# Inverse roots of two layer norms, moved from GpSimd's power to ScalarE's logarithm and exponential with a Newton step on VectorE

## The chip, the cores and the metric

The kernel runs on one core of one Trainium2 chip. The metric is device time in microseconds (us), the median of several runs; less is better. Engines go by the names of the profile: PE (TensorE), PEld (its weight loads), DVE (VectorE), ACT (ScalarE), POOL (GpSimd), SP (SyncE). L714 is line 714 of the kernel before.

## The reference

One decoder block without causal mask on 8 sequences of 512 tokens, width 192, in float32:

```python
params = quantum_params[token_ids.reshape(-1)]        # gather: 36 angles per token
ev = _circuit_expvals(params)                         # 6-qubit circuit, 6 expectations
h = (ev @ post_w.T + post_b).reshape(b, s, -1)
h = h + attention(_layernorm(h), W_qkv, b_qkv)        # one head, softmax over 512 keys
h = h + experts(_layernorm(h), Wg, W1, b1, W2, b2)    # top 2 of 8 experts, hidden 384, exact gelu
# _layernorm(x) = (x - mean) / sqrt(var + 1e-5)
```

Two layer norms per token are computed, so two inverse roots 1 / sqrt(var + 1e-5) per token are wanted.

## The kernel before, in words

A token's embedding is a linear map of 6 expectations, so the kernel never forms it for attention: it works with 7 to 15 numbers per token ("features") and small matrices that are folded from the weights at the start. Tokens lie 128 to a tile; there are 32 tiles, 4 per sequence (a "batch" b of 0 to 7). Two chunks of 16 tiles (batches 0 to 3 and 4 to 7) go through the circuit.

**The start.** POOL gathers the angles, one indirect DMA per tile (`gather_angles`, L542): 16 tiles for chunk 0, later 16 for chunk 1 in pieces. DVE reduces the angles, ACT takes sine and cosine (`trig`, three pieces p), DVE (chunk 0) or DVE and POOL (chunk 1, `pair_strings` on POOL) multiply the circuit out to `ev`.

**First norm.** Per chunk c, `variance1(c)` on DVE leaves var + eps in `ve1` (L1173, semaphore `var1_done`). POOL's `rstd1(p)` raises it to the power -0.5 (L714), in four parts p of 4, 12, 4 and 12 tiles. DVE's `features(p)` waits for that (`rs1_done`), scales and writes `u` and `w`, from which PE makes keys (`keys`), queries and the factor (`factor`, waits for `w_done`) of the batch. Ahead of `features(0)` DVE computes `form(0, 0, E)` (L1156, L1160), which needs no root.

**Attention.** Per batch and half h, PE multiplies scores (L1862 for maxima, L1855 transposed for the softmax), DVE takes maxima (`row_max`, L1191), ACT exponentiates (`softmax`, L1593), PE multiplies the context (L1874), DVE divides (`context`).

**Second norm and routing.** Per batch, `variance2(b)` on DVE copies PE's gram product (L1240, semaphore `t2_copied`) and leaves `ve2` (L1248). For batches 0 to 2 (`POWERS` is 3) POOL's `rstd2(b)` raises it to -0.5 (L718); for batches 3 to 7 DVE starts from a bit trick and takes three Newton steps (`route_and_root`, with `root_square`, `root_scale`, `root_next` at L1272, L1275, L1278). `normed(b)` uses the root (L1339, L1340), ACT's `gap_exponent` and DVE's `shares(b)` give the gates (L1220, `gates_done`), and POOL scatters 8 tiles of rows per batch to HBM by indirect DMA (`scatter`, L725), batch after batch.

**Experts.** SP loads 71 blocks of 128 rows back, PE multiplies up (L2084) and down (L2096), ACT applies gelu (L1720) and the share (L1732), POOL scatters each block's result (L770), SP loads the sums, DVE adds them.

The order on each engine is the order of the calls, written out by hand; each engine runs its queue in order, and a wait holds all that is behind it. On POOL the order around the change is: 4 gathers, `last_string(0)`, 7 gathers, `rstd1(0)`, `rstd1(1)`, 5 gathers, `pair_strings(1)` with `rstd2(0)` inside it, then the scatters of batch 0 with `rstd1(2)`, `rstd1(3)` between them, `rstd2(1)` ahead of its second half and `rstd2(2)` in batch 1, then all other scatters, then the 71 scatters of results. PE's `residual(0, 0)` (L1941), which stands ahead of scores of batches 4 and 5 in PE's queue, waits for `t2_copied` to reach 4, which is `variance2(3)`.

## Time and profile before

| what | value |
|---|---|
| median of 3 runs | 297.35 us |
| lowest and highest run | 296.71 and 297.77 us |
| span of the profiled execution | 294.9 us |
| busy share of the span: PE, DVE, ACT, POOL | 72%, 59%, 41%, 71% |

The span is the time from the first to the last instruction of the one execution that the profiler recorded; no separate time of that execution is given. The median of the runs is 2.45 us above the span; that is taken as what lies around it. Busy shares are averages over stages with different limits: the start, attention with routing (about 55 to 160 us), and the experts (160 us to the end).

### The profile page before, as it was taken

What the parts mean: (1) busy time and instruction counts of PE and PEld (TensorE: products, weight loads), DVE (VectorE), ACT (ScalarE), POOL (GpSimd) and SP (SyncE); (2) the same over time, 40 slices, a digit from 0 to 9 for tenths busy, and PEclk for the clock granted to TensorE, in tenths of its full rate; (3) what the DMA queues carried; (4) which work ended last, traced back from release to release, by engine and by line L of the source; (5) the groups of instructions that cost most, each with busy time, mean ns of one, the idle gap of its engine ahead of it and who ended that gap; (6) DMA issues with size and microseconds to landing.
All of it is one profiled execution on the core that took longest, in us unless ns stands there. A gap on an engine that the chain in (4) does not pass through costs nothing.

```text
span 294.9 us, 5764 instructions
## 1 busy us (share of the span) xinstructions
PE 211.9 (72%) x1552; PEld 150.7 (51%) x1552; DVE 175.2 (59%) x687; ACT 121.3 (41%) x292; POOL 210.2 (71%) x281
## 2 busy tenths in 40 slices
PE   0760699367864678977689598999999999988000
PEld 0540554122431434544356387878789989867000
DVE  5754999756899989595887757784211000842122
ACT  2002013135351331356533467667665766745000
POOL 5777786740899697877776776777777777777750
PEclk9999999655596655579855779999999999999655
DMA  7811003994000000000012221022333315997454
GB/s 166 278 18 15 1 3 118 397 328 163 2 0 0 4 9 11 13 13 17 14 22 47 60 45 26 16 85 86 100 101 89 96 67 175 370 364 234 111 222 161
DMA packets 25659, 29.86 MB, mean 101 GB/s; under 512 B 15130, under 2 KB 19473, under 8 KB 25435
## 3 DMA queue, kind: packets, MB, share of 16 engines
q1 hardware_dynamic: 19148, 21.54, 23.3%
q0 software_dynamic: 6480, 7.94, 8.8%
q8 instruction: 14, 0.23, 0.4%
q14 instruction: 17, 0.14, 0.2%
HBM read 14.13 MB, written 16.02 MB: 102 GB/s over the span
## 4 chain that ended last, share of the span: by engine, by line
PE 47%; DVE 21%; POOL 12%; issue 7%; ACT 7%; DMA 4%; POOLq 1%; DVEq 0%; SPq 0%; ACTq 0%
PE bank_b L2096 24%; PE bank_a L2084 6%; POOL circuit L542 5%; PE bank_b L1855 4%; PE bank_a L1862 3%; POOL shares_out L770 3%; DVE nmax L1191 3%; POOL rs L714 2%; PE bank_c L1874 2%; ACT prob L1593 2%; POOL routed L725 1%; DMA angle_stages<-shares_out 1%; PE bank_d L1958 1%; DVE circuit L883 1%; DMA shares_out<-circuit,up 1%
## 5 line engine op out<-in xcount | busy, mean ns | idle before, releaser
L770 POOL DMA_INDIRECT shares_out<-circuit,up x71 | 72.6, 1023 | 21.6 <-issue 16.5
L2096 PE MATMUL bank_b<-wide,up 128*128 x426 | 81.0, 339 | 2.8 <-ACT up L1720 1.2
L725 POOL DMA_INDIRECT routed<-rows,slot x64 | 63.3, 989 | 23.5 <-issue 18.9
L2096 PEld LDWEIGHTS bank_b<-wide,up 128*128 128x128 f32 x426 | 69.7, 194 | 9.9 <-issue 8.3
L1732 ACT ACTIVATE circuit<-bank_b,up 128x192 f32<-128x192 f32 x71 | 29.9, 421 | 25.0 <-PE bank_b L2096 23.4
L542 POOL DMA_INDIRECT circuit<-angles,ids x32 | 31.3, 978 | 10.8 <-issue 9.0
L1720 ACT ACTIVATE up<-bank_a 128x384 f32<-128x384 f32 x71 | 34.5, 489 | 6.9 <-PE bank_a L2084 6.9
L1862 PE MATMUL bank_a<-keys_t,wt 32*128 32x512 f32 x64 | 27.8, 956 | 4.7 <-DVE nmax L1191 3.0
L1855 PE MATMUL bank_b<-queries_t,keys_t 32*128 32x512 f32 x64 | 24.6, 850 | 6.2 <-ACT keys_t L1571 3.5
L1518 DVE TENSOR_TENSOR hres<-hres,prob 128x384 f32<-128x384 f32 x12 | 6.2, 559 | 37.8 <-DMA prob<-shares_out 37.7
L1191 DVE TENSOR_REDUCE nmax<-bank_a 128x2 f32<-128x1024 f32 x16 | 19.5, 1220 | 11.3 <-PE bank_a L1862 11.3
L1540 DVE COPY up<-wide 32x384 f32 x43 | 17.0, 395 | 12.6 <-PE bank_a L2084 8.3
L1593 ACT ACTIVATE prob<-bank_b 128x1024 f32<-128x1024 f32 x16 | 16.4, 1023 | 16.3 <-PE bank_b L1855 16.3
L2084 PE MATMUL bank_a<-xt,up 32*128 32x128 f32 x330 | 14.7, 309 | 1.4 <-ACT up L1720 1.3
L2084 PEld LDWEIGHTS bank_a<-xt,up 32*128 32x128 f32 x330 | 12.2, 205 | 5.3 <-issue 5.0
L1559 ACT ACTIVATE circuit<-angle_stages 128x480 f32<-128x480 f32 (+2 forms) x3 | 2.3, 780 | 28.3 <-DVE angle_stages L839 28.3
L1874 PE MATMUL bank_c<-prob,u 128*32 128x128 f32 x256 | 12.9, 366 | 0.7 <-ACT prob L1593 0.5
L1874 PEld LDWEIGHTS bank_c<-prob,u 128*32 128x32 f32 x256 | 9.5, 146 | 4.9 <-issue 2.3
L1540 DVE COPY circuit<-wide 32x384 f32 x16 | 6.2, 385 | 9.4 <-PE bank_a L2084 4.7
L1855 PEld LDWEIGHTS bank_b<-queries_t,keys_t 32*128 32x128 f32 x64 | 7.0, 251 | 9.1 <-issue 7.7
L1567 ACT COPY wide<-bank_a 128x384 f32<-128x384 f32 x8 | 3.8, 478 | 18.2 <-PE bank_a L1800 18.2
L1862 PEld LDWEIGHTS bank_a<-keys_t,wt 32*128 32x128 f32 x64 | 7.1, 267 | 7.4 <-issue 4.8
(433 smaller groups left out, 392.9 us busy)
## 6 DMA issues: line engine op xcount, KB each, us to landing
routed<-pad_rows SPq DMA_DIRECT2D x8, 528.0 KB, 5.2
out<-hres SPq DMA_DIRECT2D x7, 384.0 KB, 6.0
wide<-down_w SPq DMA_DIRECT2D x1, 2304.0 KB, 12.6
prob<-shares_out SPq DMA_DIRECT2D x3, 768.0 KB, 5.4
up<-up_w SPq DMA_DIRECT2D x1, 1536.0 KB
angle_stages<-shares_out SPq DMA_DIRECT2D x2, 768.0 KB, 7.0
form_p<-shares_out SPq DMA_DIRECT2D x2, 768.0 KB, 7.1
up<-routed SPq DMA_DIRECT2D x71, 16.0 KB, 1.7
```

The lines of the kernel that those rows point to most:

```text
L542: pool.indirect_dma_start(out=theta_all[:, t, :], out_offset=None, in_=angles, in_offset=bass.IndirectOffsetOnAxis(ids[:, b, j:j + 1], 0)) ...
L725: pool.indirect_dma_start(out=routed, out_offset=bass.IndirectOffsetOnAxis(slot[:, b, k, j:j + 1], 0), in_=rows[:, b, k, j, :], in_offset=None
L770: pool.indirect_dma_start(out=shares_out, out_offset=bass.IndirectOffsetOnAxis(xb[:, m, DEST:DEST + 1].bitcast(I32), 0), in_=y[:, m % RESU ...
L1191: dve.tensor_reduce(nmax[:, b % 2, 2 * h:2 * h + 2], bank_a[:, 0:2, :], AX.X, ALU.max, negate=True).then_inc(max_done, 1)
L1540: copied = dve.tensor_copy(up_now[s % UP_TILES][r, :], wide_flat[r, bass.ds(first + HC * D, HID)])
L1720: act.activation(hid[:, n, :], bank_a[:, n, 0:HID], ACT.Gelu).then_inc(gelu_done, 1)
L1732: act.mul(y[:, m % RESULTS, :], bank_b[:, m % 2, 0:D], xb[:, m, SHARE:SHARE + 1]).then_inc(y_done, 1)
L1855: mm = pe.matmul(bank_b[:, n, :], keys_t[r, bt % 3, k * P:(k + 1) * P], queries_t[r, :], start=True, stop=True)
L1862: mm = pe.matmul(bank_a[:, n, :], wt[r, bs % 2, :], keys_t[r, bs % 3, :], start=True, stop=True)
L1874: mm = pe.matmul(bank_c[j * F:(j + 1) * F, 0:P], u[:, b * TILES + k, :], prob[:, k, j * P:(j + 1) * P], start=(k == 0), stop=(k == TILES - 1),
L2084: mm = pe.matmul(bank_a[:, n, c * P:(c + 1) * P], weights[r, c * P:(c + 1) * P], xt[r, 0, :], start=True, stop=True)
L2096: mm = pe.matmul(bank_b[:, m % 2, 0:D], hid[:, m % STEP, c * P:(c + 1) * P], wide_flat[:, bass.ds(first + c * D, D)], start=(c == 0), stop ...
```

## The change

POOL's powers go (`rstd1`, `rstd2`, `minus_half`). ACT gets `root1(c)`, once per chunk, and `root2(b)` for batches 0 to 2: the logarithm of var + eps, then exp(-0.5 of it). DVE gets functions of the same names that wait for ACT's value and take one Newton step of three chained instructions each. The gathers of chunk 1 on POOL now stand in one run of 12. ACT loads a table set with both functions after `trig(0)` and after `trig(2)`.

```diff
             gather_angles(COUNT[0], COUNT[0] + GATHERS_EARLY)
             join()
             constants()
             last_string(0)
-            gather_angles(COUNT[0] + GATHERS_EARLY, ANGLE_LAST[1])
-            rstd1(0)
-            rstd1(1)
-            gather_angles(ANGLE_LAST[1], T)
-            pair_strings(1, lambda: rstd2(0))
+            gather_angles(COUNT[0] + GATHERS_EARLY, T)
+            pair_strings(1)
             pool.wait_ge(pads_out, 16 * (E + 1))
             for b in range(BATCHES):
-                if b == 0:
-                    scatter(0, 0, 0, 2)
-                    rstd1(2)
-                    scatter(0, 0, 2, TILES)
-                    rstd1(3)
-                else:
-                    scatter(b, 0)
-                if b + 1 < POWERS:
-                    rstd2(b + 1)
+                scatter(b, 0)
                 scatter(b, 1)
...
+            def root1(c):
+                n = COUNT[c]
+                dve.wait_ge(rs1_done, c + 1)
+                step(dve.tensor_tensor(square1[:, 0:n], rs1[:, 0:n], rs1[:, 0:n], ALU.mult))
+                join()
+                step(dve.scalar_tensor_tensor(square1[:, 0:n], square1[:, 0:n], -0.5, ve1[:, 0:n], ALU.mult, ALU.mult))
+                join()
+                step(dve.scalar_tensor_tensor(rs1[:, 0:n], square1[:, 0:n], 1.5, rs1[:, 0:n], ALU.add, ALU.mult))
+                join()
...
+            def root2(b):
+                dve.wait_ge(rs2_done, b + 1)
+                root_square()
+                join()
+                root_scale()
+                join()
+                root_next()
...
             form(0, 0, E)
+            root1(0)
             features(0)
...
             route(0)
+            root2(0)
             normed(0)
...
             form(1, 0, E)
+            root1(1)
             features(2)
             route(1)
             features(3)
+            root2(1)
             normed(1)
...
             row_max(5, 0)
+            root2(2)
             normed(2)
...
+            def root1(c):
+                n = COUNT[c]
+                act.wait_ge(var1_done, c + 1)
+                act.activation(log1[:, 0:n], ve1[:, 0:n], ACT.Ln).then_inc(log1_done, 1)
+                act.wait_ge(log1_done, c + 1)
+                act.activation(rs1[:, 0:n], log1[:, 0:n], ACT.Exp, scale=-0.5).then_inc(rs1_done, 1)
...
             trig(0)
+            act.preload_act_table_set("natural_log_exp_and_others")
             for e in range(E):
                 up_copy(e)
+            root1(0)
             spread_u(0)
...
                     trig(2)
+                    act.preload_act_table_set("natural_log_exp_and_others")
...
             at_copy(1)
+            root2(0)
             softmax(2, 1)
...
             softmax(3, 0)
+            root1(1)
             at_copy(2)
+            root2(1)
             softmax(3, 1)
...
             context_copy(3)
+            root2(2)
```

How the order moves on DVE at the first norm, before (L1173 is `variance1`'s last step, L1156 and L1160 are `form(0, 0, E)`, L1182 opens `features(0)` and then `features(1)`):

```order
L1173 TENSOR_SCALAR ve<-var_s 128x16 [waits dve_step]
L1156 TENSOR_TENSOR form_p<-ev,form_w 128x16x56
L1160 TENSOR_REDUCE form_s<-form_p 128x16x8 [waits dve_step]
L1182 TENSOR_TENSOR u<-ev,rs 128x4x7 [waits rs1_done,dve_step]
L1184 TENSOR_TENSOR form_s<-form_s,rs 128x4x8
L1186 TENSOR_TENSOR w<-form_s,form_w 128x4x8 [waits dve_step]
L1182 TENSOR_TENSOR u<-ev,rs 128x12x7 [waits rs1_done]
```

and now:

```order
L1154 TENSOR_SCALAR ve<-var_s 128x16 [waits dve_step]
L1137 TENSOR_TENSOR form_p<-ev,form_w 128x16x56
L1141 TENSOR_REDUCE form_s<-form_p 128x16x8 [waits dve_step]
L1160 TENSOR_TENSOR square<-rs 128x16 [waits rs1_done,dve_step]
L1162 SCALAR_TENSOR_TENSOR square<-square,ve 128x16 [waits dve_step]
L1164 SCALAR_TENSOR_TENSOR rs<-square,rs 128x16 [waits dve_step]
L1173 TENSOR_TENSOR u<-ev,rs 128x4x7 [waits dve_step]
L1175 TENSOR_TENSOR form_s<-form_s,rs 128x4x8
L1177 TENSOR_TENSOR w<-form_s,form_w 128x4x8 [waits dve_step]
L1173 TENSOR_TENSOR u<-ev,rs 128x12x7
```

Three chained instructions now stand ahead of `features(0)`, and `features(1)` waits for no other engine any more.

On DVE at batch 2, before (two maxima L1191 and the copy L1198 between them, then `normed(2)`, then L1240, the copy of `variance2(3)`):

```order
L1191 TENSOR_REDUCE nmax<-bank_a 128x2 [waits s_done]
L1198 COPY w_rep<-nmax 128x16 [waits queries_done,max_done]
L1191 TENSOR_REDUCE nmax<-bank_a 128x2 [waits s_done]
L1339 TENSOR_TENSOR gap<-gap,rs 128x4 [waits rs2_done]
L1340 TENSOR_TENSOR rows<-ev,rs 128x8x15
L1240 COPY t<-bank_a 128x96 [waits t2_done]
```

and now:

```order
L1182 TENSOR_REDUCE nmax<-bank_a 128x2 [waits s_done]
L1189 COPY w_rep<-nmax 128x16 [waits queries_done,max_done]
L1182 TENSOR_REDUCE nmax<-bank_a 128x2 [waits s_done]
L1263 TENSOR_TENSOR square<-rs 128x4 [waits rs2_done]
L1266 SCALAR_TENSOR_TENSOR scaled<-square,ve 128x4 [waits dve_step]
L1269 SCALAR_TENSOR_TENSOR rs<-scaled,rs 128x4 [waits dve_step]
L1336 TENSOR_TENSOR gap<-gap,rs 128x4 [waits dve_step]
L1337 TENSOR_TENSOR rows<-ev,rs 128x8x15
L1231 COPY t<-bank_a 128x96 [waits t2_done]
```

The Newton step of batch 2 stands ahead of the copy that `residual(0, 0)` on PE waits for.

On ACT around the second piece of angles, now (before, the list is the same without the row ACT_TABLE_LOAD and without `log` and `rs`):

```order
L1629 ACTIVATE log<-ve 128x16 [waits var1_done]
L1631 ACTIVATE rs<-log 128x16 [waits log1_done]
L1614 COPY u_rep<-u 128x16x9 [waits u_done]
L1577 COPY wt<-bank_a 128x128 [waits wt_done]
L1573 COPY keys_t<-bank_d 128x512 [waits keys_done]
L1561 ACT_TABLE_LOAD
L1561 ACTIVATE circuit<-angle_stages 128x30x11 [waits reduced]
```

The table load of the sine stands ahead of the wait for the angles (`reduced`), so it may run while that wait is still open.

## Rows read from the trace of the kernel before

**Rows 1.** The page, part 4: chain that ended last, by engine.

```profile
PE 47%; DVE 21%; POOL 12%; issue 7%; ACT 7%; DMA 4%; POOLq 1%; DVEq 0%; SPq 0%; ACTq 0%
```

**Rows 2.** Lines L714 and L718: count, ns min/median/max, first and last start.

```profile
L714 POOL TENSOR_TENSOR rs<-ve,minus_half x4: 1051/2048/2304, 52.7 to 107.0; 128x4 f32<-128x4 f32 x2, 128x12 f32<-128x12 f32 x2
...
L718 POOL TENSOR_TENSOR rs<-ve,minus_half x3: 997/1042/1044, 94.0 to 120.4; 128x4 f32<-128x4 f32 x3
```

**Rows 3.** Timeline, POOL: start us, us, what, [idle before and its releaser].

```profile
158.81 0.95 POOL L725 DMA_INDIRECT routed<-rows,slot  x1 [1.73 <-DVE ev L1220]
...
179.91 0.97 POOL L725 DMA_INDIRECT routed<-rows,slot  x1 [1.22 <-issue]
...
283.78 1.22 POOL L770 DMA_INDIRECT shares_out<-circuit,up  x1 [0.30 <-issue]
```

**Rows 4.** Timeline, DVE: the last instruction of two batches' shares.

```profile
157.81 0.19 DVE L1220 TENSOR_TENSOR ev<-shared 128x32 f32<-128x32 f32 x1
...
178.92 0.19 DVE L1220 TENSOR_TENSOR ev<-shared 128x32 f32<-128x32 f32 x1
```

**Rows 5.** Timeline, DVE: a Newton step by itself, and the instruction behind it.

```profile
129.53 0.16 DVE L1272 TENSOR_TENSOR square<-rs 128x4 f32<-128x4 f32 x1
129.73 0.16 DVE L1275 SCALAR_TENSOR_TENSOR scaled<-square,ve 128x4 f32<-128x4 f32 x1
...
130.12 0.16 DVE L1339 TENSOR_TENSOR gap<-gap,rs 128x4 f32<-128x4 f32 x1
```

**Rows 6.** Timeline, ACT.

```profile
59.80 0.80 ACT L1559 ACTIVATE circuit<-angle_stages 128x330 f32<-128x330 f32 x1 [2.45 <-DVE angle_stages L839]
...
71.35 1.28 ACT L1593 ACT_TABLE_LOAD   x1
...
96.65 0.20 ACT L1628 ACTIVATE gap_e<-gap 128x4 f32<-128x4 f32 x1
```

**Rows 7.** Timeline, DVE, first norm of chunk 0.

```profile
49.83 0.98 DVE L1156 TENSOR_TENSOR form_p<-ev,form_w 128x784 f32<-128x784 f32 x1
...
52.55 1.08 DVE L1156 TENSOR_TENSOR form_p<-ev,form_w 128x896 f32<-128x896 f32 x1
...
54.79 0.19 DVE L1182 TENSOR_TENSOR u<-ev,rs 128x28 f32<-128x28 f32 x1
...
56.84 0.25 DVE L1182 TENSOR_TENSOR u<-ev,rs 128x84 f32<-128x84 f32 x1 [1.51 <-POOL rs L714]
...
60.22 1.22 DVE L1191 TENSOR_REDUCE nmax<-bank_a 128x2 f32<-128x1024 f32 x1
```

**Rows 8.** Timeline, PE: the first scores.

```profile
57.40 2.08 PE L1862 MATMUL bank_a<-keys_t,wt 32*128 32x512 f32 x4 [0.67 <-ACT keys_t L1571]
```

**Rows 9.** Timeline, DVE, first norm of chunk 1 and batch 1.

```profile
108.20 0.22 DVE L1268 TENSOR_REDUCE both<-both 128x8 bf16<-128x40 bf16 x1
109.30 0.25 DVE L1182 TENSOR_TENSOR u<-ev,rs 128x84 f32<-128x84 f32 x1 [0.88 <-POOL rs L714]
...
110.28 0.16 DVE L1339 TENSOR_TENSOR gap<-gap,rs 128x4 f32<-128x4 f32 x1 [0.20 <-POOL rs L718]
...
113.23 1.21 DVE L1191 TENSOR_REDUCE nmax<-bank_a 128x2 f32<-128x1024 f32 x1
```

**Rows 10.** Timeline, PE: scores behind that maximum, and the residual of batch 0.

```profile
114.59 2.08 PE L1862 MATMUL bank_a<-keys_t,wt 32*128 32x512 f32 x4 [0.89 <-DVE nmax L1191]
...
121.35 1.06 PE L1835 MATMUL bank_d<-ident,w_rep 128*128 128x128 f32 x4
122.48 1.01 PE L1941 MATMUL bank_a<-m,a2t 32*128 32x192 f32 x4
```

**Rows 11.** Timeline, DVE: the copy of the second norm of batch 3.

```profile
122.13 0.25 DVE L1240 COPY t<-bank_a 128x96 f32<-128x96 f32 x1
```

**Rows 12.** Timeline, POOL and DVE side by side.

```profile
90.46 1.70 POOL L688 TENSOR_TENSOR pair_e<-pair_e,turn 128x720 f32<-128x720 f32 x1
90.51 1.76 DVE L1084 TENSOR_TENSOR z_exp<-z_exp,circuit 128x96 f32<-128x96 f32 x1
```

More of the change, by code:

```diff
@@ L74, in build @@
     FEATURE_LAST = [sum(FEATURE_BATCHES[:p + 1]) for p in range(len(FEATURE_BATCHES))]
-    POWERS = CHUNK_BATCHES[0] - 1
+    GUESSED = CHUNK_BATCHES[0] - 1
     USED = ANGLES - QUBITS
@@ L153, in build @@
         ones_b = sb("ones_b", [P, P], BF16)
-        minus_half = sb("minus_half", [P, CT])
         exp_i = sb("exp_i", [P, E], I32)
@@ L202, in build @@
         rs1 = sb("rs1", [P, CT])
+        log1 = sb("log1", [P, CT])
+        square1 = sb("square1", [P, CT])
+        log2 = sb("log2", [P, TILES])
         w = sb("w", [P, T, F])
@@ L314, in build @@
         rs1_done = sem("rs1_done")
+        log1_done = sem("log1_done")
+        log2_done = sem("log2_done")
         u_done = sem("u_done")
@@ L544, in gather_angles @@
                                             ).then_inc(angles_in[p], 16)
-            step(pool.memset(minus_half[:, :], -0.5))
             pool.wait_ge(ids_in, 16)
@@ L608, in last_string, with pair_strings @@
                 pool.tensor_tensor(of(x_exp, n)[:, 5], lc[:, 0, 0], lc[:, 0, 1], ALU.add).then_inc(last_done, 1)
-            def pair_strings(c, between):
+            def pair_strings(c):
                 n = COUNT[c]
@@ L694, in pair_strings @@
                 pjoin()
-                between()
                 pool.tensor_tensor(d[:, :, 0], g[:, :, 0, 0], s[:, :, 1], ALU.add)
@@ L708, in pair_strings @@
                 pool.tensor_tensor(x, x, sin_of(c, 2, 0), ALU.mult).then_inc(pairs_done, 1)
-            def rstd1(p):
-                c, first, last = part_tiles(p)
-                own = slice(first - TILE0[c], last - TILE0[c])
-                pool.wait_ge(var1_done, c + 1)
-                pool.tensor_tensor(rs1[:, own], ve1[:, own], minus_half[:, own], ALU.pow).then_inc(rs1_done, 1)
-            def rstd2(b):
-                pool.wait_ge(var2_done, b + 1)
-                pool.tensor_tensor(rs2[:, :], ve2[:, :], minus_half[:, 0:TILES], ALU.pow).then_inc(rs2_done, 1)
             def scatter(b, k, first=0, last=TILES):
@@ L1180, in features @@
                 scale = rs1[:, own].unsqueeze(2)
-                dve.wait_ge(rs1_done, p + 1)
                 dve.tensor_tensor(u[:, tiles, 0:PU], ev[:, tiles, 0:PU], scale.to_broadcast([P, n, PU]), ALU.mult
@@ L1334, in normed @@
             def normed(b):
-                if b < POWERS:
-                    dve.wait_ge(rs2_done, b + 1)
-                else:
-                    join()
+                join()
                 dve.tensor_tensor(gap_2[:, :], gap[:, :], rs2[:, :], ALU.mult).then_inc(gap_done, 1)
@@ L1622, in spread_w, with root2 @@
                          ).then_inc(w_spread, 1)
+            def root1(c):
[4 more added lines that the diff above has]
+                act.activation(rs1[:, 0:n], log1[:, 0:n], ACT.Exp, scale=-0.5).then_inc(rs1_done, 1)
+            def root2(b):
+                act.wait_ge(var2_done, b + 1)
+                act.activation(log2[:, :], ve2[:, :], ACT.Ln).then_inc(log2_done, 1)
+                act.wait_ge(log2_done, b + 1)
+                act.activation(rs2[:, :], log2[:, :], ACT.Exp, scale=-0.5).then_inc(rs2_done, 1)
             def gap_exponent(b):
```

## Prediction

> **What bounds the kernel now.** I read the page's chain of waits first. It gives POOL 12% of the span [rows 1], and much of that share in its middle belongs to the powers that the change removes. That invites a large gain, so the next view is the powers' own lines: seven of them, 1.0 to 2.3 us each [rows 2]. But a long instruction on POOL costs only what somebody waits for it, so the third view is DVE's timeline, where the users of the roots stand. DVE idled for a power 1.51 us at `features(1)` [rows 7], 0.88 us at `features(3)` and 0.20 us at `normed(1)` [rows 9]. The other four powers end before their users come. That is 2.59 us in all: the stock from which a gain can come.
>
> The second thing to see is how the end is set. The last scatter of results starts at 283.78 us and the first scatter of batch 7 at 179.91 [rows 3]; 8 + 71 scatters in 103.9 us, 78 steps of 1.33 us, and the timeline shows none of them idle for more than about 0.3 us ahead. So from 179.91 on POOL itself is the limit. What lets it begin is DVE: the shares of batch 7 end at 178.92 + 0.19 = 179.11 [rows 4], and the scatter follows 0.80 us later. Batch 5 shows the same with the releaser named: shares end at 158.00 [rows 4], scatter at 158.81 after 1.73 us of idle [rows 3]. POOL is therefore waiting for the attention path at 158 and again at 179. Time that the powers free on POOL around 103 to 121 us only makes these waits longer. What counts is how far the path DVE, PE, ACT through attention shifts.
>
> **The change part by part.** All positions are those of the profiled execution, span 294.9 us; the median of the runs is 2.45 us above, which I carry over unchanged.
>
> *The new steps.* A Newton step standing by itself: first instruction at 129.53, the instruction behind it at 130.12 [rows 5], so 0.59 us for three chained instructions. The width (16 instead of 4 columns for the first norm) adds at most some hundredths. Lower bound: the three busy times of about 0.16 us without gaps, 0.48 us. Upper bound: one of the steps held by POOL as in [rows 12], where an instruction of 96 columns took 1.76 us beside a POOL instruction of 1.70 us. I take 0.59, from the row of the very same instructions. There are five steps, 2.95 us of DVE.
>
> *ACT's pair.* The trace shows no logarithm. The nearest row is an exponential of 4 columns, 0.20 us [rows 6]; the upper bound is a sine of 330 columns, 0.80 us [rows 6]. I take 0.20 each, by width, and about 0.5 us for the pair with its hand-over. Cover at the first norm: the power starts at 52.7 [rows 2], so the pair can start there and be done by 53.3 (54.4 at the upper bound), while DVE works without a gap until 54.79 [rows 7]. Free. Were the cover gone, `features(0)` would pay the 0.5 us. In chunk 1 and for batches 0 to 2 the pair stands in ACT's queue at a place where its input is ready within half a microsecond, and DVE reads the result microseconds later (route and features lie between), so it is free there too; behind it wait small copies and a softmax that itself waits for PE.
>
> *Tables.* Two more loads. One row costs 1.28 us [rows 6]. The one after `trig(0)` falls into an empty ACT. The sine's load falls behind the first key copy, which ends just ahead of the first scores [rows 8], so at about 58.0 us now, and ACT idled 2.45 us at this place for the angles [rows 6]; 58.0 + 1.28 is before the 59.8 at which the sine starts now. Free. The load after `trig(2)` takes the place of the one at 71.35, same length. Zero.
>
> *Gathers in one run.* The last five, issued from 57 us on, now come without the pause; DVE does not wait for any gather there, before or after. Zero. POOL's pair products start when DVE allows it, as before. Zero.
>
> *First norm, chunk 0.* DVE's Newton step delays `features(0)` from 54.79 to 55.38. PE's factor, keys and first scores follow: 57.40 becomes 57.99, ending 2.08 later at 60.07 [rows 8]. On the other side `features(1)` starts at 56.84 - 1.51 + 0.59 = 55.92 [rows 7], 0.92 us early, and with it the reduction of angles, so DVE would be ready for the first maximum at 60.22 - 0.92 = 59.30 [rows 7]. The maximum needs both: about 60.1 instead of 60.22. **-0.1 us.** The 1.51 us of waiting is nearly all lost again: DVE now waits for PE.
>
> *Chunk 1 and batches 0, 1.* Between about 82 and 113 us the timeline shows no idle time of DVE but the two waits, so it is the path. Three steps come in (`root2(0)`, `root1(1)`, `root2(1)`): 3 x 0.59 = 1.77. Two waits go: 0.88 + 0.20 = 1.08 [rows 9]. **+0.7 us** at the maximum of 113.23 [rows 9]. PE idles 0.89 us for just that maximum before 114.59 [rows 10]; PE's own work there is later by two steps, 1.2 us, so it would be ready at 114.9, and the maximum allows 115.2. DVE stays the last, and the shift passes on.
>
> *Batch 2.* `root2(2)` stands ahead of the copy at 122.13 + 0.25 = 122.38 [rows 11]. PE is free for the residual at 121.35 + 1.06 = 122.41 and starts it at 122.48 [rows 10]: there is no slack, and scores of batches 4 and 5 are queued behind it. The step passes on whole. **+0.6 us.** The power it replaces was not waited for.
>
> *POOL.* Four powers leave the stretch of scatters, but the waits of [rows 3] take that in. **0.**
>
> Sum: -0.1 + 0.7 + 0.6 = +1.2 us. Everything behind 122 us is chained to that residual, the same as before. 294.9 + 1.2 is 296.1 of span, 298.5 us of time.
>
> Waits are not all that a power can cost DVE. The product of 896 columns beside the first power took 1.08 us, that of 784 columns without any POOL arithmetic 0.98 us [rows 7], 1.21 and 1.25 ns a column; a power of a few columns does not slow DVE visibly. [rows 12] show that a wide POOL product does. The Trainium skill, page "Advanced Engine Details and Errata", section "VectorE Performance Modes", says that VectorE's second port to SBUF is shared with GPSIMD and that the two block each other. By that rule, with the powers holding the port, taking them away would free DVE time as well; what it gives is the first rival. The row at 52.55 disagrees with it for these narrow powers, the row at 90.51 agrees for a wide one.
>
> **The rivals.**
>
> 1. *Faster: the powers hold DVE.* In chunk 1 powers of 1.05 and 2.30 us [rows 2] run beside DVE work; less the 0.88 us in which DVE idled anyway, up to 2.5 us of DVE could come back there. +1.2 - 2.5 = -1.3: about 296.1 us. For it: [rows 12]. Against it: the two rates in [rows 7]. It decides if DVE's instructions from 103 to 109 us run clearly shorter than before.
> 2. *Absorbed.* One of the two shifts meets slack that I do not see: the residual's scores matter less than the maxima of batch 5, or PE hides a part at 114.6. Then only +0.6: 297.9 us, no measurable change. For it: margins of 0.1 to 0.3 us in my comparisons. Against it: PE idles for DVE in [rows 10].
> 3. *Slower still: a Newton step is held by POOL.* `root2(0)` comes at about 96 us while POOL's pair products still run. A hold as at 90.51 [rows 12], 1.76 us where a product of 84 columns takes 0.25 [rows 7], so 1.5 us, would give +2.7: 300.0 us. It decides if one of the new instructions shows far above 0.2 us. Against it: the wide product is over by then.
>
> That the change does not do what it says is excluded by the order of instructions.
>
> **How the numbers follow.** A measurement of this kernel tells about 0.3%, 0.9 us, from no change: the bounds are 296.5 and 298.2 us. My forecast has 0.50, with its own range 297.8 to 299.2 (steps of 0.48 to 0.7 us, and 0.5 us for the spread of the runs): 0.35 of it slower, 0.15 the same. Rival 1 has 0.18: 0.15 faster, 0.03 the same. Rival 2 has 0.17: 0.16 the same, 0.01 slower. Rival 3 has 0.15, all slower. Together: faster 0.15, same 0.34, slower 0.51. The range from 296.4 to 300.0 leaves out most of rival 1 and the outer part of rival 3, under 2 in 10.
>
> **What would show it.** Right: `features(1)` no longer waits, but the first maximum stands at 60.1 with DVE idle ahead of it for PE; the pair on ACT done by 53.3 and 0.2 us each; five Newton steps of 0.6 us; the maximum of 113.23 about 0.6 later, the residual of batch 0 about 1.2 later, the first scatter of batch 7 about 181.1, POOL's idle time ahead of the scatters of batches 1, 2 and 5 larger; from there the same 79 scatters. Wrong: the first maximum a microsecond early, DVE's instructions beside the former powers shorter, the residual not behind the copy, or another start of batch 7 than the path says.

## The result and the profile after

The changed kernel took 298.81 us in the median of 4 runs (298.08 to 301.14); the kernel before, run beside it on the same chip, 297.03. The ratio on record is 1.0101, with a 95% interval of 1.0052 to 1.0150 (it is taken over the executions and is not the quotient of these two medians, 1.006). Measured once more (label new_again below) it is 1.0111 (1.0068 to 1.0154). By the means of this study, over 11 executions of the changed kernel and 145 of the kernel before, it is 299.43 against 296.28 us: **+3.1 us**. Executions more than 1.5% above the fastest of the same kernel count as disturbed and are left out of every mean here. The forecast was +1.2, and 298.5 in all. The direction was right and the time lies in the range; the size of the change was forecast at well under half. That 298.81 lies so near 298.5 is in part luck: the forecast started from a median of three, 297.35, which is 1.1 us above the mean of the 145, and this hid half of the miss.

The page of the changed kernel; compare the chain with [rows 1]. The third line is TensorE's granted clock in 40 slices of 7.4 us (9 is full, 5 is half).

```profile
PE 209.3 (70%) x1552; PEld 150.1 (50%) x1552; DVE 178.2 (60%) x702; ACT 125.9 (42%) x304; POOL 200.4 (67%) x273
...
PEclk9999997555975755559955579999999999999655
...
PE 48%; DVE 26%; POOL 8%; issue 7%; ACT 6%; DMA 4%; POOLq 0%; DVEq 0%; SPq 0%; ACTq 0%
```

POOL's share of the chain fell from 12% to 8%: the powers have left it, and yet the kernel is slower. The span of this execution is 297.6 us and its time 299.32, so 1.72 us lie around the span. That is also so in the other executions (1.72 to 1.76 us in the mean of each kernel). The prediction took 2.45, the median less the span of one execution, and so started 0.7 us too high.

The first norm on DVE, which answers to [rows 7] (start, length, engine, line, operation, tiles, count, idle time before it and its releaser):

```profile
52.41 1.08 DVE L1137 TENSOR_TENSOR form_p<-ev,form_w 128x896 f32<-128x896 f32 x1
...
54.65 0.18 DVE L1160 TENSOR_TENSOR square<-rs 128x16 f32<-128x16 f32 x1
54.87 0.18 DVE L1162 SCALAR_TENSOR_TENSOR square<-square,ve 128x16 f32<-128x16 f32 x1
55.08 0.18 DVE L1164 SCALAR_TENSOR_TENSOR rs<-square,rs 128x16 f32<-128x16 f32 x1
55.29 0.19 DVE L1173 TENSOR_TENSOR u<-ev,rs 128x28 f32<-128x28 f32 x1
...
55.75 0.24 DVE L1173 TENSOR_TENSOR u<-ev,rs 128x84 f32<-128x84 f32 x1
...
60.03 1.22 DVE L1182 TENSOR_REDUCE nmax<-bank_a 128x2 f32<-128x1024 f32 x1 [0.65 <-PE bank_a L1884]
```

The step takes 55.29 - 54.65 = 0.64 us; `features(1)` (55.75) waits for nothing, and the first maximum stands at 60.03 with DVE idle for PE. This is what the prediction said, to a tenth. ACT's side of it, for the first norm (and the sine's table load, which was to come at 58.0):

```profile
52.54 0.22 ACT L1629 ACTIVATE log<-ve 128x16 f32<-128x16 f32 x1 [4.73 <-DVE ve L1154]
52.79 0.22 ACT L1631 ACTIVATE rs<-log 128x16 f32<-128x16 f32 x1
...
57.88 1.28 ACT L1561 ACT_TABLE_LOAD   x1
```

The pair is done at 53.01. The load hides in ACT's wait for the angles but for some 0.3 us: DVE has the angles ready at 58.85 now, and the sine starts at 59.17, still 0.63 earlier than in [rows 6]. Now chunk 1, batches 0 and 1 on DVE, against [rows 9], with the POOL row beside the first of them:

```profile
95.02 0.70 DVE L1269 SCALAR_TENSOR_TENSOR rs<-scaled,rs 128x4 f32<-128x4 f32 x1
...
108.49 0.23 DVE L1173 TENSOR_TENSOR u<-ev,rs 128x84 f32<-128x84 f32 x1
...
109.18 0.15 DVE L1263 TENSOR_TENSOR square<-rs 128x4 f32<-128x4 f32 x1
...
109.56 0.16 DVE L1269 SCALAR_TENSOR_TENSOR rs<-scaled,rs 128x4 f32<-128x4 f32 x1
109.76 0.16 DVE L1336 TENSOR_TENSOR gap<-gap,rs 128x4 f32<-128x4 f32 x1
...
112.47 1.22 DVE L1182 TENSOR_REDUCE nmax<-bank_a 128x2 f32<-128x1024 f32 x1
```

```profile
95.01 0.69 POOL L703 TENSOR_TENSOR pair_d<-pair_d,turn 128x240 f32<-128x240 f32 x1
```

Both waits for powers are gone. The maximum of batch 4 stands at 112.47, 0.76 us earlier than in [rows 9], where the prediction had 0.6 later. And the third instruction of `root2(0)` takes 0.70 us instead of 0.16, beside a POOL product of 0.69. Last, PE's residual, against [rows 10], and POOL's first scatters of batches 5 and 7, against [rows 3]:

```profile
122.32 0.69 PE L1963 MATMUL bank_a<-m,a2t 32*128 32x192 f32 x2 [0.65 <-issue]
```

```profile
160.74 0.96 POOL L717 DMA_INDIRECT routed<-rows,slot  x1 [1.67 <-DVE ev L1211]
...
182.48 0.98 POOL L717 DMA_INDIRECT routed<-rows,slot  x1 [1.67 <-issue]
```

The residual stands 0.16 us earlier than in the first trace of before, the first scatter of batch 7 is 2.57 us later (182.48 against 179.91). Most of the loss thus shows behind the place where the prediction had stopped counting. From the first scatter of batch 7 to the last scatter of results it is 104.06 us, against 103.87 before, so next to nothing is lost there. One recorded execution of each kernel does not tell whether that is the change or the execution, so both were recorded again.

### The profile page after: what moved, and what is told of

Same layout as the page of the kernel before. It is cut to its first block, busy times and chain, and to the rows that moved or that the text cites. A ratio compares the mean times of both kernels' runs of the same rounds, so it can differ in the third digit from the quotient of the medians.

```text
span 297.6 us, 5781 instructions
## 1 busy us (share of the span) xinstructions
PE 209.3 (70%) x1552; PEld 150.1 (50%) x1552; DVE 178.2 (60%) x702; ACT 125.9 (42%) x304; POOL 200.4 (67%) x273
## 4 chain that ended last, share of the span: by engine, by line
PE 48%; DVE 26%; POOL 8%; issue 7%; ACT 6%; DMA 4%; POOLq 0%; DVEq 0%; SPq 0%; ACTq 0%
PE bank_b L2118 24%; PE bank_a L2106 6%; POOL circuit L546 5%; PE bank_a L1884 4%; PE bank_b L1877 4%; POOL shares_out L751 3%; DVE nmax L1182 3%; PE bank_c L1896 2%; DVE form_s L1141 1%; DVE circuit L864 1%; DVE form_p L1137 1%; PE bank_d L1835 1%; PE bank_d L1857 1%; DVE circuit L870 1%; DVE circuit L861 1%
## 5 line engine op out<-in xcount | busy, mean ns | idle before, releaser
L1884 PE MATMUL bank_a<-keys_t,wt 32*128 32x512 f32 x64 | 27.2, 935 | 3.3 <-ACT keys_t L1573 1.7
L1877 PE MATMUL bank_b<-queries_t,keys_t 32*128 32x512 f32 x64 | 23.9, 827 | 5.1 <-ACT keys_t L1573 2.7
L1182 DVE TENSOR_REDUCE nmax<-bank_a 128x2 f32<-128x1024 f32 x16 | 19.5, 1220 | 11.5 <-PE bank_a L1884 11.5
L1542 DVE COPY up<-wide 32x384 f32 x43 | 16.4, 381 | 12.8 <-PE bank_a L2106 8.3
L1896 PE MATMUL bank_c<-prob,u 128*32 128x128 f32 x256 | 13.7, 384 | 0.8 <-ACT prob L1595 0.7
L1847 PE MATMUL bank_a<-ident,w 128*128 128x128 f32 x8 | 3.4, 420 | 12.6 <-DVE w L1177 10.3
L1857 PE MATMUL bank_d<-ident,w_rep 128*128 128x128 f32 x32 | 7.5, 382 | 4.7 <-issue 4.7
```

The costliest lines, as they stand in the source:

```text
L1182: dve.tensor_reduce(nmax[:, b % 2, 2 * h:2 * h + 2], bank_a[:, 0:2, :], AX.X, ALU.max, negate=True).then_inc(max_done, 1)
L1542: copied = dve.tensor_copy(up_now[s % UP_TILES][r, :], wide_flat[r, bass.ds(first + HC * D, HID)])
L1877: mm = pe.matmul(bank_b[:, n, :], keys_t[r, bt % 3, k * P:(k + 1) * P], queries_t[r, :], start=True, stop=True)
L1884: mm = pe.matmul(bank_a[:, n, :], wt[r, bs % 2, :], keys_t[r, bs % 3, :], start=True, stop=True)
L1896: mm = pe.matmul(bank_c[j * F:(j + 1) * F, 0:P], u[:, b * TILES + k, :], prob[:, k, j * P:(j + 1) * P], start=(k == 0), stop=(k == TILES - 1),
```

## The experiments

L numbers are those of the kernel meant. "Mean" is over the executions of a kernel, with a standard error of 0.2 to 0.5 us; the kernel before has 296.28. The runs were spread over five chips, on which the kernel before had means of 296.1 to 296.6, so means of different chips are compared below.

| kernel | ratio to before, 95% interval | mean, us (executions) |
|---|---|---|
| old_again | 1.0012 (0.9984 to 1.0041) | with before |
| old_third | 0.9981 (0.9945 to 1.0016) | with before |
| new_again | 1.0111 (1.0068 to 1.0154) | 299.43 (11, with the first 4) |
| no_newton | 0.9961 (0.9927 to 0.9996) | 295.31 (12) |
| newton_twice | 1.0204 (1.0156 to 1.0252) | 302.80 (6) |
| only_first | 0.9994 (0.9965 to 1.0022) | 295.90 (12) |
| only_chunk1 | 1.0082 (1.0049 to 1.0114) | 298.29 (7) |
| only_batch2 | 0.9991 (0.9960 to 1.0022) | 295.87 (12) |
| only_batch0 | 0.9976 (0.9934 to 1.0019) | 295.76 (8) |
| only_root1_1 | 0.9995 (0.9962 to 1.0028) | 296.06 (12) |
| only_batch1 | 0.9965 (0.9932 to 0.9998) | 294.83 (12) |
| only_two | 0.9989 (0.9958 to 1.0020) | 296.01 (11) |
| root2_earlier | 1.0064 (1.0033 to 1.0096) | 297.80 (9) |
| old_with_steps | 1.0076 (1.0042 to 1.0110) | 298.47 (11) |
| idle_power | 1.0075 (1.0037 to 1.0114) | 298.75 (10) |
| log_for_more | 0.9936 (0.9898 to 0.9973) | 294.99 (12) |

### Both kernels again: old_again, new_again, old_third

No edit. What was expected, of old_again and new_again, and later of old_third:

> The kernel before, unchanged, measured against itself. All theories: ratio 1.000 within 0.003. What it tells is TensorE's granted clock: the profiled execution of the kernel before had 0.822 over its span, the changed one 0.806, and the changed one's trace loses 1.5 to 2 us between 122 and 175 us where the clock stands at its lower level for longer. Theory 'clock by chance': the executions of this kernel spread over 0.80 to 0.82, and those at about 0.805 are about 1.5 us longer. Theory 'clock by the kernel': all executions of this kernel lie at about 0.82.

> The changed kernel, unchanged, measured again. Theory 'steps alone' (what is lost is the Newton steps on VectorE's path, +1.2 us as forecast; the rest of the first measurement was chance of the executions): ratio 1.002 to 1.006, clocks spread as in the kernel before. Theory 'steps and clock' (the shifted work loses granted clock in every execution): ratio 1.008 to 1.012 again, clocks at 0.80 to 0.806 in nearly all.

> The kernel before once more, for the trace. Theory 'the waits for powers in chunk 1 were an accident of the first recorded execution': no idle time of VectorE for a power at features(3) and normed(1), as in the second one (there 0.20 us at normed(0) alone). Rival 'they are usual': 0.5 to 1.1 us of idle time there.

The change's loss came back whole (1.0111), so it is no chance of one measurement. Time at full clock, worked out per execution from its span and mean clock (the lower level counts 0.5, so it is the span times twice the clock less one), is 186 us in the mean of the kernel before (granted 0.799 to 0.828) and 182 in that of the changed one. That the kernel before always stands at 0.82 is wrong; it spreads, and its 25 executions at 0.806 or less took 297.6 us in the mean, the other 120 296.0. The seven of new_again lie at 0.806 to 0.812, above the 0.80 to 0.806 that 'steps and clock' had.

The theory of an accident fell with old_third. DVE in old_third, then in old_again, at the same place of the program:

```profile
94.93 0.32 DVE L1339 TENSOR_TENSOR gap<-gap,rs 128x4 f32<-128x4 f32 x1 [0.20 <-POOL rs L718]
...
108.56 0.25 DVE L1182 TENSOR_TENSOR u<-ev,rs 128x84 f32<-128x84 f32 x1 [0.87 <-POOL rs L714]
109.55 0.16 DVE L1339 TENSOR_TENSOR gap<-gap,rs 128x4 f32<-128x4 f32 x1 [0.20 <-POOL rs L718]
```

```profile
94.83 0.32 DVE L1339 TENSOR_TENSOR gap<-gap,rs 128x4 f32<-128x4 f32 x1 [0.20 <-POOL rs L718]
...
102.39 0.18 DVE L1204 RECIPROCAL rinv<-bank_c 128x4 f32<-128x4 f32 x1 [0.66 <-PE bank_c L1881]
```

Two of three recorded executions wait 1.07 or 1.08 us for the powers of these two places; the third does not, and 6 us earlier it has waited 0.66 us for PE's context. (The two later recordings also wait 0.20 us for a power at `normed(0)`, where the first trace has no wait.) Here is what differs: two stretches by engine, first in old_third, then in old_again (busy time and count of PE, PEld, DVE, ACT, POOL, then granted clock, DMA share, GB/s):

```profile
100.00:103.50 3.50, 2.39 (x14) 0.82 (x10) 3.23 (x11) 1.55 (x3) 3.00 (x3) 0.97 0.04 9
121.70:130.50 8.80, 6.66 (x40) 3.77 (x40) 7.72 (x47) 4.85 (x12) 6.67 (x8) 0.69 0.06 13
```

```profile
100.00:103.50 3.50, 2.74 (x8) 0.75 (x8) 2.60 (x9) 1.29 (x2) 2.98 (x4) 0.50 0.04 9
120.90:129.60 8.70, 6.49 (x40) 3.76 (x40) 7.62 (x47) 4.62 (x12) 6.57 (x8) 0.70 0.05 11
```

Around 101 us old_third had a short **bout at 2.4 GHz** (0.97), old_again ran at 1.2 (0.50). With the bout PE's context comes early and the power is what DVE waits for; without it DVE waits for PE first, and the power is done in time. All 18 recorded executions of this study bear this out: in none of the 8 with this bout does DVE wait for PE at that reciprocal, and in 9 of the 10 without it it waits 0.65 to 0.88 us. The 1.08 us of [rows 9] were worth that much only in executions with that bout. The second row of each is the stretch from `residual(0, 0)` to `row_max(6, 0)`: both have a bout in it. The same two stretches in the changed kernel, first the execution on the page, then new_again:

```profile
100.00:103.50 3.50, 2.59 (x22) 0.93 (x14) 3.23 (x12) 2.08 (x6) 2.89 (x3) 0.96 0.04 9
122.30:131.90 9.60, 7.42 (x40) 4.39 (x40) 7.42 (x47) 4.27 (x11) 5.17 (x7) 0.50 0.04 9
```

```profile
100.00:103.50 3.50, 2.93 (x17) 0.75 (x9) 2.46 (x8) 1.20 (x3) 2.89 (x3) 0.50 0.04 9
123.40:133.00 9.60, 7.44 (x40) 4.34 (x40) 7.44 (x48) 4.25 (x11) 5.17 (x7) 0.51 0.04 9
```

So with the early bout there are the first trace of before, old_third and the page of after; without it there are old_again and new_again. Cut at DVE's and PE's rows into stretches, A from `row_max(3, 0)` to `row_max(4, 0)`, B to `residual(0, 0)`, C to `row_max(6, 0)`, D to the end of `shares(7)`, in us:

| execution | A (bout near 101) | B | C (bout in it) | D (bout at 150 to 168) |
|---|---|---|---|---|
| before, first trace | 26.87 (yes) | 9.25 | 8.96 (yes) | 47.67 (yes) |
| old_third | 27.59 (yes) | 9.25 | 8.78 (yes) | 46.87 (yes) |
| old_again | 26.93 (no) | 8.88 | 8.74 (yes) | 46.96 (yes) |
| after, the page | 28.08 (yes) | 9.85 | 9.59 (no) | 49.77 (no) |
| new_again | 28.47 (no) | 9.84 | 9.60 (no) | 47.03 (yes) |
| no_newton | 26.16 (no) | 9.64 | 9.59 (no) | 49.11 (no) |
| only_two | 26.88 (yes) | 9.26 | 8.86 (yes) | 48.06 (yes) |

Where both have the bout, A costs +0.49 against old_third (28.08 - 27.59) and +1.21 against the first trace (28.08 - 26.87); where neither has it, +1.54 (28.47 - 26.93). Two executions of the same kernel with the bout differ by 0.72 themselves, so the bout alone does not set this cost. B costs +0.60 against the two traces without a bout in it. C is 9.59 us without a bout and 8.74 to 8.96 with one. D is 2 to 3 us longer in the page of after than in new_again or the kernel before; that execution has no bout there. In the mean of the recorded executions (three before, two after) the residual comes at 121.70 and 122.85, +1.15, and `shares(7)` ends at 177.69 and 180.84, +3.15.

### All steps out, or twice: no_newton, newton_twice

```diff
 def root1(c):
...
     dve.wait_ge(rs1_done, c + 1)
-    step(dve.tensor_tensor(square1[:, 0:n], rs1[:, 0:n], rs1[:, 0:n], ALU.mult))
...
 def root2(b):
...
     dve.wait_ge(rs2_done, b + 1)
-    root_square()
...
-    root_next()
```

newton_twice has these lines twice instead.

> The changed kernel without its five Newton steps: the roots are ScalarE's exponentials of -0.5 times the logarithm as they stand; the refinement is left out. Theory 'steps alone': first norm 0.65 us earlier than before the change (first maximum at about 59.55), the two waits of 0.88 and 0.20 us gone without steps in their place, batch 2 unchanged: 0.9 to 1.7 us faster than the kernel before, ratio 0.994 to 0.997. Theory 'clock' (what was lost behind 122 us doesn't hang on the steps): 0 to 1 us slower than before, ratio 1.000 to 1.004. Theory 'logarithm and tables on ScalarE': first maximum no earlier than before, ratio 1.003 or more.

> The changed kernel with each Newton step done twice, 2.95 us of VectorE more. Theory 'steps alone': chunk 0 +0.6, chunk 1 and batches 0 and 1 +1.8, batch 2 +0.6, together 2.4 to 3.0 us more than the changed kernel, ratio to the kernel before 1.012 to 1.016 if the changed one has 1.004. Theory 'clock': the shift passes 122 us as 2.4 to 3.0 but the end is off it by up to 2 us either way, with the granted clock.

Without steps the kernel is 1.0 us faster than before, at the near end of what was expected; the first maximum stands at 59.55, as expected to the hundredth. So no cost of the ACT pair, the tables and the gathers shows, and five steps cost 299.43 - 295.31 = 4.1 us where they are 2.95 us of DVE (error 0.5). The second five cost 3.4 more. That is above the 2.4 to 3.0 of 'steps alone' but within its error; 'clock' allowed it at the end, yet not that the shift is above 3.0 already at `residual(0, 0)`, which newton_twice has at 126.68 where the changed kernel has it at 122.32 and 123.37. The steps are the whole loss, and all five together cost more than themselves. That the rest of the gain from the waits was not to be had shows in DVE's rows of no_newton:

```profile
59.55 1.23 DVE L1176 TENSOR_REDUCE nmax<-bank_a 128x2 f32<-128x1024 f32 x1 [0.88 <-PE bank_a L1873]
...
101.35 0.18 DVE L1189 RECIPROCAL rinv<-bank_c 128x4 f32<-128x4 f32 x1 [0.65 <-PE bank_c L1892]
...
114.52 1.22 DVE L1176 TENSOR_REDUCE nmax<-bank_a 128x2 f32<-128x1024 f32 x1 [0.37 <-PE bank_a L1873]
```

A faster DVE waits for PE: 0.88 us for the first scores, 0.65 us for the context and 0.37 us for the scores of `row_max(4, 1)`.

### Steps one by one: only_first, only_batch2, only_chunk1

The edit puts a condition ahead of the step's lines, or takes them out where no step is wanted; only_first, for example (it has no step in `root2`):

```diff
 def root1(c):
...
     dve.wait_ge(rs1_done, c + 1)
-    step(dve.tensor_tensor(square1[:, 0:n], rs1[:, 0:n], rs1[:, 0:n], ALU.mult))
...
+    if c in (0,):
+        step(dve.tensor_tensor(square1[:, 0:n], rs1[:, 0:n], rs1[:, 0:n], ALU.mult))
...
```

> The changed kernel with the Newton step of chunk 0 alone; the other four are left out, so those roots are not refined. Without any step the first maximum came at 59.55 us, with all of them at 60.14. Theory 'each step costs itself': first maximum at 60.1, the whole 0.6 us longer than without any step, ratio to the kernel before 0.997 to 0.999. Theory 'clock' (a shift is turned into a larger or smaller one by the granted clock behind it): the shift at the first maximum is 0.6, at the end anything from -1 to +2, ratio 0.993 to 1.003.

> The changed kernel with the steps of chunk 1 and of batches 0 and 1 alone; chunk 0's and batch 2's are left out. Theory of the forecast (three steps of 0.59 less two waits of 1.08 us that a power really cost): +0.7 us against the kernel before less the 0.6 of chunk 0, so ratio 1.000 to 1.001. Theory 'the waits were an accident of the one recorded execution' (in the second recorded execution of the kernel before, features(3) and normed(1) wait for no power): the three steps cost 1.8 us and the 0.5 us for which a product on GpSimd holds one of them, so +2.3 us at the maximum of batch 4 against no step at all, some 0.4 of it hidden by TensorE behind it: ratio 1.002 to 1.004.

> The changed kernel with the Newton step of batch 2 alone; the other four are left out. Without any step the ratio was 0.996. Theory 'it passes on whole, once': +0.6 us at residual(0, 0) and at the end, ratio 0.997 to 0.999. Theory 'it is worth more than itself' (moving it ahead of row_max(5, 0) took 1.6 us off the changed kernel by the means of 9 and 11 executions): +1.6 us, ratio 1.000 to 1.003.

Chunk 0's step costs 295.90 - 295.31 = 0.6 us, batch 2's 0.6 us, as the forecast had them. The three of chunk 1 and of batches 0 and 1 cost 298.29 - 295.31 = 3.0 us (error 0.4): this is the term that was wrong, and more than either theory had for it. 0.6 + 0.6 + 3.0 = 4.2 agrees with the 4.1 of all five.

### The three apart: only_batch0, only_root1_1, only_batch1, only_two

The same edit with other conditions; only_two has `root1(1)` and `root2(1)`.

> The changed kernel with the Newton step of batch 0's second norm alone; the others are left out. Without any step the mean was 295.3 us. Theory 'the GpSimd product holds this step': third instruction 0.70 us, row_max(3, 1) 1.1 us later, mean 296.4 us, ratio 0.999 to 1.001. Rival 'each of the three costs the same third of 3.0 us': mean 296.3 us too, but then with 0.6 us at row_max(3, 1) and the rest behind it. Rival 'each costs itself, the excess comes when they add up': mean 295.9 us.

> The changed kernel with the Newton step of the first norm of chunk 1 alone; the others are left out. Theory 'the excess is the product on GpSimd, at batch 0 alone': +0.6 us against no step, mean 295.9 us, ratio 0.997 to 0.999. Rival 'each of the three costs a third of 3.0 us': mean 296.3 us. TensorE would still be free to hide some: 0.4 us of slack stood behind the maximum of batch 4 without steps, so +0.2 us is possible.

> The changed kernel with the Newton step of batch 1's second norm alone; the others are left out. Theory 'the excess is the product on GpSimd, at batch 0 alone': +0.2 to 0.6 us against no step, mean 295.5 to 295.9 us, ratio 0.996 to 0.999. Rival 'each of the three costs a third of 3.0 us': mean 296.3 us.

> The changed kernel with the Newton steps of the first norm of chunk 1 and of batch 1's second norm alone; the other three are left out. Theory 'each costs itself, once': mean between 295.6 us (the sum of the two single runs) and 296.5 us (twice 0.59 on no step), ratio 0.996 to 0.999, time at full clock 184 to 186 us. Theory 'two steps in one stretch lose a bout of the full clock': mean 297.0 us or more, ratio 1.001 to 1.004, time at full clock 180 to 183 us, and from row_max(3, 1) to row_max(4, 0) 17.5 us without a bout at about 100 us, where one step alone shows 16.1.

The hold is there in only_batch0. Its DVE row and the POOL row beside it:

```profile
94.53 0.69 DVE L1263 SCALAR_TENSOR_TENSOR rs<-scaled,rs 128x4 f32<-128x4 f32 x1
```

```profile
94.52 0.69 POOL L703 TENSOR_TENSOR pair_d<-pair_d,turn 128x240 f32<-128x240 f32 x1
```

`row_max(3, 1)` comes 1.1 us after that of no_newton, as the theory of the hold said; in the time it makes +0.5 us where that theory had 1.1, from only 8 of 12 executions (all 12 would make it +1.3). only_root1_1 costs 0.75, as expected; only_batch1 -0.5, where 0.2 to 0.6 was expected and the error is 0.5; only_two 0.7: two steps in one stretch cost no more than themselves, and the theory that they lose a bout fell. Batch 0 alone and these two make 0.5 + 0.7 = 1.2 us, the three together 3.0, and the error of that difference is about 0.7; with all 12 executions of only_batch0 and of only_two the excess would be 0.6 and not 1.8. So it is not settled whether the three together cost more than their sum, and where an excess would lie the single steps don't show.

### The product moved away: idle_power

Two fills of constants at the start, for the power's operands, are left out here:

```diff
 pjoin()
+pool.tensor_tensor(idle_p[:, 0:TILES], idle_p[:, CT - TILES:CT], minus_half[:, 0:TILES], ALU.pow)
 pool.tensor_tensor(d[:, :, 0], g[:, :, 0, 0], s[:, :, 1], ALU.add)
```

> The changed kernel with one idle power of 4 columns on GpSimd at the place in pair_strings where the kernel before had that of batch 0; nobody waits for its result. In the changed kernel the third instruction of root2(0) takes 0.70 us beside a GpSimd product of 240 columns (0.69 us); in the kernel before the power of 1.06 us put that product 1.1 us later. Theory 'the product holds the step': with the power back, the third instruction takes about 0.2 us, row_max(3, 1) starts 0.5 us earlier, and the whole is about 0.5 us faster than the changed kernel, ratio to the kernel before 1.008 to 1.010 where the changed one has 1.011. Rival 'the step is long for another reason': 0.70 us as before, nothing won.

DVE and POOL of idle_power:

```profile
94.53 0.15 DVE L1268 TENSOR_TENSOR square<-rs 128x4 f32<-128x4 f32 x1
...
94.91 0.23 DVE L1274 SCALAR_TENSOR_TENSOR rs<-scaled,rs 128x4 f32<-128x4 f32 x1
```

```profile
93.72 1.07 POOL L702 TENSOR_TENSOR idle_p<-idle_p,minus_half 128x4 f32<-128x4 f32 x1
...
96.14 0.69 POOL L708 TENSOR_TENSOR pair_d<-pair_d,turn 128x240 f32<-128x240 f32 x1
```

The mechanism is shown: a power that nobody needs puts the product 1.1 us later, the step is back from 0.70 to 0.23 us, and `row_max(3, 1)` starts at 95.57 instead of 96.03, 0.5 us earlier as expected. The step's first instruction (94.53) lies wholly beside the power and takes 0.15 us, as in the changed kernel. The mean is 0.7 us below that of the changed kernel, from 10 of 12 executions (all 12 would make it 0.2), ratios 1.0075 and 1.0111; the intervals overlap, so the time agrees with the 0.5 us expected and does not prove it.

### Batch 2's step in DVE's wait: root2_earlier

```diff
-            row_max(5, 0)
             root2(2)
+            row_max(5, 0)
             normed(2)
```

> The changed kernel with root2(2) on VectorE ahead of row_max(5, 0), for which VectorE waits 2.6 us. Theory of the forecast: the step disappears in the wait, residual(0, 0) and all behind it come 0.6 us earlier, ratio to the kernel before 1.007 to 1.010 where the changed kernel has 1.011. Rival 'TensorE is late there anyway': residual(0, 0) as in the changed kernel, ratio 1.011.

Stretch B is 9.25 us instead of 9.85: the step went into the wait, 0.6 us as forecast. The mean gained 1.6, more than that; the recorded execution has no hold at `root2(0)` (0.16 us) though nothing ahead of it was changed, so part of the 1.6 may belong to the executions (its error is 0.5).

### Steps without the change: old_with_steps

`spare(n)` has three instructions of the same kinds into tiles that nobody reads, called at the five places of the steps:

```diff
             route(0)
+            spare(TILES)
             normed(0)
```

> The kernel before with five idle chains of three small instructions on VectorE, of the same widths and at the same places as the Newton steps; the powers stay on GpSimd and give the roots. Theory 'VectorE's steps are all that the change costs': first maximum unchanged (the chain of chunk 0 fits into the wait for the second power), +1.3 to 1.8 us at the maximum of batch 4, +0.6 at residual(0, 0), the whole as slow as the changed kernel: ratio 1.008 to 1.013. Theory 'the waits are real': the chains of chunk 1 fit into 1.08 us of wait, ratio 1.003 to 1.006. Theory 'ScalarE's pair, its tables or GpSimd's scatters cost it': ratio 1.000 to 1.003.

+2.2 us with all powers still on POOL: most of the change's loss is there with nothing but DVE's instructions added. The ratio, 1.0076, falls between the first two theories. ACT's and POOL's side of the change are not needed for this much of the loss, and taking the powers away gave the changed kernel nothing against this one (299.43 against 298.47). The hold can be part of that difference: here the power stands where it stood, and the third instruction at batch 0 takes 0.22 us.

### A version that beats both: log_for_more

no_newton, and for batches 4, 5 and 6 ACT's pair in place of the bit trick and three steps. Like no_newton it leaves the refinement out, so its roots are those of the tables as they stand. DVE's side in part:

```diff
+                if b not in LOGGED:
                     root_square()
...
+                if i - 2 in LOGGED:
+                    root2(i - 2)
                 normed(i - 2)
```

> A version that may beat both: the changed kernel without Newton steps, and with ScalarE's logarithm and exponential for batches 4, 5 and 6 too, in place of the bit trick and three Newton steps on VectorE; the refinement is left out. The chains of these batches interleave with the division of the context (L1312, L1317 of the changed kernel), on which TensorE waits: six small instructions of about 0.16 us lie ahead of it. Theory 'VectorE's small instructions are on the path': 0.5 to 1.0 us from batches 4 and 5 each, so 1 to 2 us faster than no step at all: ratio 0.989 to 0.993. Rival 'they are hidden behind TensorE's ranks and context': ratio 0.996 as without steps.

Ratio 0.9936 (0.9898 to 0.9973), 1.3 us faster than before and 4.4 faster than the changed kernel. Against no_newton its mean gains 0.3 us, which the errors don't separate from nothing. The first theory, 1 to 2 us faster than no step at all, did not come true. DVE's rows show why it is not more: freed of batch 4's chain, DVE waits 1.05 us for PE's ranks, where no_newton (first row) waits 0.41.

```profile
143.48 0.22 DVE L1313 TENSOR_TENSOR slot_e<-mask,bank_c 128x64 f32<-128x64 f32 x1 [0.41 <-PE bank_c L1932]
```

```profile
143.28 0.22 DVE L1322 TENSOR_TENSOR slot_e<-mask,bank_c 128x64 f32<-128x64 f32 x1 [1.05 <-PE bank_c L1949]
```

## Why the prediction was right in direction and short in size

- **The gain that the chain of waits invites** is not there: right. All powers gone and no step put in their place (no_newton) is worth 1.0 us, of 12% of the span that the chain gave POOL. Nor did "much of that share" belong to the powers: the same page's list by line has 2% for L714.
- **Newton step 0.59, ACT's pair 0.2 each, tables and gathers zero**: right (0.64 for 16 columns, 109.76 - 109.18 = 0.58 for 4; 0.22; for the last two, no_newton shows no cost). **POOL 0**: right as well, by the 104.06 and 103.87 us above.
- **First norm -0.1**: right. -0.19 against the first trace of before, 0.00 between old_again and new_again (60.14 both).
- **Batch 2 +0.6**: right. +0.60 in stretch B against the first trace and old_third, +0.6 us by only_batch2.
- **Chunk 1 and batches 0, 1: +0.7, from "Two waits go: 0.88 + 0.20"**: this step failed. The waits were read from one execution as a constant of the kernel. They stand in two of three recorded executions, those in which TensorE's clock rose near 101 us; without the rise DVE waits for PE and not for the power. In the traces the term is +0.49 or +1.21 with the rise and +1.54 without. The means say more: no_newton gains 1.0 us, of which about 0.6 stands at the first maximum (59.55 against 60.09 to 60.22), so by the end the two waits gave about 0.4 us and not 1.08 (no_newton lacks the bout in C as well); and the three steps cost 3.0 us and not 1.77 (only_chunk1), of which 0.5 is the hold below. The term by the means is then 3.0 - 0.4 = +2.6 instead of +0.7, with an error of about 0.3. It holds what these steps cost anywhere, behind 122 us too.
- **A step held by POOL**, rival 3 with a chance of 0.15, came true in part: 0.70 us instead of 0.16 in five of six recorded executions that have `root2(0)` and no idle power, and the cause is shown by idle_power. "The wide product is over by then" was read off the old order on POOL; the change itself, by taking a power of 1.06 us out from between the products, moved a product of 240 columns onto the step. The hold is 0.5 us and not the 1.5 of the rival, which took its price from a product of 720 columns. The Trainium skill ("Advanced Engine Details and Errata", section "VectorE Performance Modes") says that GPSIMD and VectorE instructions that use the shared port block each other; these rows agree for the product of 240 columns and not for the power, beside which a DVE instruction kept its 0.15 us.
- **The powers hold DVE** (rival 1) did not happen: the product of 896 columns takes 1.08 us at 52.41 with no power beside it, as it did at 52.55 with one, and in the rows that answer to those from 103 to 109 us before, the sign that rival 1 named, no DVE instruction is more than 0.02 us shorter.
- **"Everything behind 122 us is chained to that residual, the same as before"**: this failed too. At the residual the recorded executions differ by +1.15 us, about what the sum had for that place (in part by luck: A and B together are +1.9 where the sum had 1.3, and the first trace of before lost some 1.2 us against the other two ahead of `row_max(3, 0)`); by the end of `shares(7)` it is +3.15. Stretch C is 0.6 to 0.9 us longer, without a bout at 2.4 GHz that all three recorded executions of the kernel before have, and D is 1.2 us longer in the mean. What loses the bout in C is not settled. It is also missing in 14 of the 15 recorded executions of the variants and the changed kernel together, in old_with_steps (steps and powers) and in no_newton (neither) among them, so losing it needs neither the steps nor the removal of the powers; only_two has it.
- **Absorbed** (rival 2) did not happen: old_with_steps and only_batch2 show that the steps pass on.

The account by terms: by the traces, 0 for the first norm, +0.5 to +1.5 in A, +0.6 in B, +0.6 to +0.9 in C make 1.7 to 3.0 us; the rest up to the 3.1 of the means could lie in stretch D, where one recorded execution of the changed kernel lost 2 to 3 us and the other nothing. By the means, 0 + 2.6 + 0.6 = 3.2 us agrees with the 3.1. The two accounts cut the same loss in different ways; how much of it comes with the clock behind 122 us stays open. Against 296.28 + 1.2 = 297.5, what the terms of the prediction would have given on a sound base, the measured mean is 1.9 us higher.

## What to carry to other kernels

A wait that one trace shows is a difference of two arrivals, and it is worth its length only in executions in which the other one is early; record a second execution before a wait is booked as a gain. Taking an instruction off an engine moves all that stands behind it there: ask what the moved work now meets on the other engine. And a root from logarithm and exponential on an engine that has time is cheap, but refining steps on the engine that is the path cost at least their length (4.1 us for five of 0.59), unless they stand in a wait of that engine, as batch 2's did in root2_earlier.

## What was not expected of the hardware

- TensorE's clock differs from execution to execution of the same program at the same place: from 100.0 to 103.5 us it is 0.97 in one execution of the kernel before and 0.50 in another. Over whole executions it is 0.799 to 0.828. With a bout of some 3.4 us at 2.4 GHz stretch C is 0.6 to 0.9 us shorter: PE was busy 6.49 to 6.66 us of it with the bout and 7.42 to 7.44 without.
- A narrow instruction on DVE is not immune to POOL: a 4-column SCALAR_TENSOR_TENSOR took 0.70 us beside a 240-column POOL product of 0.69, and 0.16 us at batch 1 (109.56), while beside a power of 4 columns (1.07 us) a 4-column TENSOR_TENSOR kept its 0.15.
- A logarithm of 4 or 16 columns costs what an exponential does on ACT: 0.20 to 0.22 us each.
